# Multi-query attention with causal masks: where the mask is applied

## The reference

```python
Q = (x @ Wq + bq).reshape(B, S, H, Dh).transpose(0, 2, 1, 3)   # B, S = 8, 512; H, Dh = 16, 8
K = x @ Wk + bk
V = x @ Wv + bv
A = einsum('bhqd,bkd->bhqk', Q, K)
A = where(tril(ones((S, S))), A, -inf)
P = softmax(A / sqrt(Dh), axis=-1)
O = einsum('bhqk,bkd->bhqd', P, V)
return O.transpose(0, 2, 1, 3).reshape(B, S, H * Dh) @ Wo + bo
```

## Time and profile before

| | before |
|---|---|
| median of 3 runs | 4353.27 us |
| profiled execution | 4353.17 us, span 4351.2 us |
| PE, DVE, ACT, POOL busy | 3755.5, 3342.7, 2178.1, 2945.7 us |
| attention stage | about 49 to 676 us, a batch every 78.9 us |
| mean granted PE clock | 0.96 |

### The profile page before, as it was taken

How to read it: one execution, slowest core, us unless ns; L and a number is a source line. 1 busy time by engine, 2 the same in 40 slices (tenths; PEclk the granted TensorE clock), 3 DMA queues, 4 the chain that set the end, 5 groups by cost and what they waited for, 6 DMA issues and landing times. The chain is left out here.

```text
span 4351.2 us, 158059 instructions
## 1 busy us (share of the span) xinstructions
PE 3755.5 (86%) x67688; PEld 2914.4 (67%) x67880; DVE 3342.7 (77%) x4810; ACT 2178.1 (50%) x2712; POOL 2945.7 (68%) x1281
## 2 busy tenths in 40 slices
PE   6888895889888898988898988989888989889985
PEld 4555554767676776766777767777666767777773
DVE  3454555888887888887888878888878788888884
ACT  3444443555554555554555545555545555555552
POOL 1101005888887877887888878788877788788872
PEclk9999997999999999999999999999999999999997
DMA  1000001222223222222222232222222222222221
GB/s 48 3 5 2 5 3 43 77 61 61 61 62 80 57 62 61 61 66 72 61 61 62 61 80 60 61 61 60 66 73 60 61 61 62 66 62 61 61 61 50
DMA packets 162246, 239.83 MB, mean 55 GB/s; under 512 B 42258, under 2 KB 60632, under 8 KB 161496
## 3 DMA queue, kind: packets, MB, share of 16 engines
q1 hardware_dynamic: 161624, 230.00, 20.5%
HBM read 21.00 MB, written 4.19 MB: 6 GB/s over the span
## 5 line engine op out<-in xcount | busy, mean ns | idle before, releaser
L1054 POOL TENSOR_TENSOR norms<-sumsb,minus_half 128x16 f32<-128x16 f32 x384 | 1145.3, 2983 | 238.9 <-DVE sumsb L1381 212.1
L1058 POOL TENSOR_TENSOR by_cos<-by_cos,by_sin 128x1024 f32<-128x1024 f32 x384 | 917.9, 2390 | 356.9 <-DVE by_sin L1373 351.7
L1279 ACT ACTIVATE squares<-proj 128x1024 f32<-128x1024 f32 x384 | 393.9, 1026 | 743.5 <-PE proj L1121 743.5
L1064 POOL TENSOR_TENSOR by_cos<-by_cos,norms 128x1024 f32<-128x1024 f32 x384 | 743.9, 1937 | 32.6
L1371 DVE TENSOR_TENSOR by_cos<-proj,turns 128x1024 f32<-128x1024 f32 x384 | 467.9, 1218 | 300.8 <-ACT squares L1279 281.1
L1119 PE MATMUL proj<-qkv_hi,xs_hib 128*128 128x512 f32 x1152 | 528.1, 458 | 57.6 <-DVE by_sin L1373 42.3
L1377 DVE TENSOR_REDUCE sumsb<-squares 128x16 f32<-128x1024 f32 x384 | 465.1, 1211 | 11.9 <-ACT squares L1279 10.3
L1120 PE MATMUL proj<-qkv_lo,xs_hib 128*128 128x512 f32 x1152 | 471.5, 409 | 0.0
L1121 PE MATMUL proj<-qkv_hi,xs_lob 128*128 128x512 f32 x1152 | 470.8, 409 | 0.0
L1373 DVE TENSOR_TENSOR by_sin<-proj,turns 128x1024 f32<-128x1024 f32 x384 | 465.6, 1213 | 0.0
L1128 PE MATMUL ring<-ident,by_cos 128*128 128x128 f32 x3072 | 410.4, 277 | 0.0
(11 more groups left out here) (173 smaller groups left out, 7346.7 us busy)
## 6 DMA issues: line engine op xcount, KB each, us to landing
v_win<-vb SPq DMA_DIRECT2D x1152, 130.0 KB
v_win<-vb SPq DMA_DIRECT2D x768, 65.0 KB
in_qkv<-L_ffn_Wqkv SPq DMA_DIRECT2D x12, 768.0 KB
wo<-L_ffn_Wo SPq DMA_DIRECT2D x6, 512.0 KB, 4.1
x_tok<-L_attn_x SPq DMA_DIRECT2D x8, 256.0 KB, 4.6
residual<-x_tok SPq DMA_DIRECT2D x8, 256.0 KB, 2.0
o_x<-residual SPq DMA_DIRECT2D x1, 2048.0 KB, 7.9
out<-o_x SPq DMA_DIRECT2D x8, 256.0 KB, 2.3
```

The lines of the kernel that those rows point to most:

```text
L1054: nc.gpsimd.tensor_tensor(norms[:, t % 2, j, :], sums[:, t % 2, j, :], c["minus_half"][:, 0:H], ALU.pow).then_inc(e[f"{w_}_norm"].sem, 1)
L1058: nc.gpsimd.tensor_tensor(by_cos[:, j, :], by_cos[:, j, :], by_sin[:, j, :], ALU.add).then_inc(e[f"{w_}_added"].sem, 1)
L1064: nc.gpsimd.tensor_tensor(heads, heads, norms[:, t % 2, j, :].unsqueeze(2).broadcast_to([P, H, DH]), ALU.mult).then_inc(e[f"{w_}_ready"].s ...
```

## The change

The causal mask leaves PE in both products. For the maxima, `mask_qk` becomes 512 columns wide, zero but for its last 128, and DVE adds its last n columns to the score inside the instruction that takes the maximum; the masked scores go to a scratch tile `a_unused` that nothing reads. Each maximum now has a second wait, on the one two before it, and an increment of a semaphore `a_dve_ready` in front. For the transposed scores no mask is added before the exponential; when a group's 12 exponentials are done, POOL sets the part under the diagonal of the first 128 columns of each block to zero in `probs`, one selection per key tile over the 4 heads, and PE's V of key tile kt waits for selection kt. On POOL's queue group 0's selections stand before inverse deviation 2 of the batch before, group 1's before inverse deviation 0, and group 3's behind `keys_again`. One selection and one memset less build the constants.

```diff
-            sp.wait_ge(selected, 9)
+            sp.wait_ge(selected, 8)
...
-            select(c["mask_qk"][:, :], [[-1, P]], ALU.is_ge, 0, MASKED, 1)
-            select(c["mask_kq"][:, :], [[1, P]], ALU.is_ge, 0, MASKED, -1)
+            select(c["mask_qk"][:, S - P:S], [[-1, P]], ALU.is_ge, 0, MASKED, 1)
...
+            def causal(b, g):
+
+                pool.wait_ge(e["exp"].sem, e["exp"].at(3 * PER_GROUP * (g + 1), b))
+                pool.sem_inc(pool_ready, 1)
+                for kt in range(TILES):
+                    own = probs[:, g % 2, :, PROB_AT[kt]:PROB_AT[kt] + P]
+                    nc.gpsimd.affine_select(out=own, in_=own, compare_op=ALU.is_ge, fill=0.0, base=0,
+                                            pattern=[[0, PER_GROUP], [1, P]], channel_multiplier=-1)\
+                        .then_inc(e["causal"].sem, 1)
+
             def sequence(b, first=False, last=False):
                 if not first:
                     inverse_deviation(1, b - 1)
+                causal(b, 0)
+                if not first:
                     inverse_deviation(2, b - 1)
+                causal(b, 1)
                 if not last:
                     inverse_deviation(0, b + 1)
+                causal(b, 2)
+                if not last:
                     keys_again(b + 1)
+                causal(b, 3)
...
-                nc.tensor.matmul(out[:, 0:n], qT0[:, g, qt * P:(qt + 1) * P], kT[:, i, 0:n], start=True, stop=False)
-                nc.tensor.matmul(out[:, n - P:n], ident_bf[:, :], c["mask_qk"][:, :],
-                                 start=False, stop=True).then_inc(e["s_full"].sem, 1)
+                nc.tensor.matmul(out[:, 0:n], qT0[:, g, qt * P:(qt + 1) * P], kT[:, i, 0:n], start=True,
+                                 stop=True).then_inc(e["s_full"].sem, 1)
...
-                    nc.tensor.matmul(out[:, at:at + n], kT1[:, i, kt * P:(kt + 1) * P], qT1[:, g, kt * P:S],
-                                     start=True, stop=False)
-                    last = nc.tensor.matmul(out[:, at:at + P], ident_bf[:, :], c["mask_kq"][:, :],
-                                            start=False, stop=True)
+                    last = nc.tensor.matmul(out[:, at:at + n], kT1[:, i, kt * P:(kt + 1) * P], qT1[:, g, kt * P:S],
+                                            start=True, stop=True)
...
             def weighted_values(b, g, kt):
 
+                pe.wait_ge(e["causal"].sem, e["causal"].at(TILES * g + kt + 1, b))
                 if kt == 0:
-                    pe.wait_ge(e["exp"].sem, e["exp"].at(3 * PER_GROUP * (g + 1), b))
...
                     dve.wait_ge(e["s_full"].sem, e["s_full"].at(s + 1, b))
-                    nc.vector.tensor_reduce(row_max[:, qt, h:h + 1], score[s % 2][:, 0:P * (qt + 1)], AX.X,
-                                            ALU.max).then_inc(e["s_max"].sem, 1)
+                    dve.wait_ge(e["s_max"].sem, e["s_max"].at(s - 1, b))
+                    dve.sem_inc(dve_ready, 1)
+                    n = P * (qt + 1)
+                    nc.vector.tensor_tensor_reduce(unused[:, s % 2, 0:n], score[s % 2][:, 0:n], c["mask_qk"][:, S - n:S], 1.0,
+                                                   LOWEST, ALU.add, ALU.max, accum_out=row_max[:, qt, h:h + 1])\
+                        .then_inc(e["s_max"].sem, 1)
```

More of the change, by code:

```diff
@@ L43 @@
 QK_SCALE = 8.0
+LOWEST = float(np.finfo(np.float32).min)
 MASKED = -1e30
@@ L112, in _ @@
             nc.vector.memset(c["mask_qk"][:, :], 0.0)
-            nc.vector.memset(c["mask_kq"][:, :], 0.0)
             nc.vector.memset(c["mask_win"][0:WINDOW, :], 0.0)
@@ L176, in mqa_events @@
         "st_full": Events(sem("a_st_full"), 3 * MQA_H), "exp": Events(sem("a_exp"), 3 * MQA_H),
+        "causal": Events(sem("a_causal"), TILES * GROUPS),
         "pv_full": Events(sem("a_pv_full"), GROUPS), "pv": Events(sem("a_pv"), GROUPS),
@@ L214, in mqa_stage @@
         o, y = sb("a_ob", [P, TILES, D]), sb("a_yb", [P, TILES, D])
-        carrier = sb("a_carrier", [P, 1])
+        carrier, unused = sb("a_carrier", [P, 1]), sb("a_unused", [P, 2, S], BF16)
         turn = [bank("a_turn0"), bank("a_turn1")]
@@ L222, in mqa_stage @@
         stored = ctx.enter_context(nc.semaphore("a_stored"))
+        pool_ready = ctx.enter_context(nc.semaphore("a_pool_ready"))
+        dve_ready = ctx.enter_context(nc.semaphore("a_dve_ready"))
         block = ctx.enter_context(nc.Block())
@@ L1573, in program @@
             "ones": sb("ones", [P, P]), "mean_of": sb("mean_of", [P, P]), "minus_half": sb("minus_half", [P, H]), "least": sb("least", [P, 2, H]),
-            "mask_qk": sb("mask_qk", [P, P], BF16), "mask_kq": sb("mask_kq", [P, P], BF16),
+            "mask_qk": sb("mask_qk", [P, S], BF16),
             "mask_win": sb("mask_win", [P, 512], BF16), "mask_first": sb("mask_first", [P, 512], BF16),
```

## The result

The changed kernel takes 4380.77 us, the median of 8 runs (4371.25 to 4397.99), against 4355.05 us before on the same chip; the ratio is 1.0054, 95% interval [1.0033, 1.0074]. It is slower, by half a percent. The forecast was 4372 us, slower with a chance of 0.60. The profiled execution took 4386.02 us, its span is 4384.1.

The account below looks back on a forecast made before the run. By busy shares PE bounds the attention cycle, though timelines show PE and DVE alternating over two score banks. Per cycle -4.3+5.4+1.45 = +2.55; with the ends +18.8 on 4353.17 us, forecast 4372 us, range 4325 to 4425.

Parts of the forecast that it names:

- part 1: Mask matmuls taken off PE in the attention stage: 4.3 us a cycle gained.
- part 3: Selections on POOL: hidden except in group 3 at the batch boundary, where V starts late: +1.45 us a cycle.
- part 2: Mask inside DVE's maximum, with readout, second wait and increment: 5.4 us a cycle lost.
- rival 3: PE, left idle longer at the batch boundary, stays at half clock for more 4-us slices: 4380 to 4400 us; chance 0.12.
- rival 1: Faster: DVE's readout, waits and increment cost nothing; cycle -2.85 us, with the ends -25, 4328 us; chance 0.28.
- a: Extra DVE time per maximum for the separate 128x1 result: 0.06 us, bounds 0 and 0.18.
- w: Second wait and increment before each maximum, counting where DVE stands ready for a score: 0.20 us, bounds 0 and 0.4.
- with nothing else changed: Condition under which PE's gains from removed masks were summed along the attention stage's path, 4.3 us a cycle.
- Rival 4: Masks cost PE next to nothing on any path, weight loads being the bound: gain 1.5 instead of 4.3, 4392 us; chance 0.06.
- Holds no edited line: The span outside the attention stage, some 3675 us, has no edited line, so the change can touch only some 630 us.
- Rival 2: Much slower by DVE: readout 0.18 us, wait and increment 0.4; cycle +10, in all +78, 4431 us; chance 0.12.
- the pair at 0.38: Sign: time from a 512-column matmul with its mask to the next, 0.38 us, becomes about 0.23 where PE is busy.

Follow-up runs that it names:

- plain_max: The changed kernel with DVE's maximum as a plain reduction, without mask, second wait or increment; 4316.74 us, ratio to before 0.9921.
- pm_keep_T: Against before, only the score mask is left out, maximum a plain reduction; transposed mask stays on PE, nothing on POOL; 4473.97 us, ratio 1.0276.
- pool_only: The changed kernel with the score mask back on PE and the plain maximum on DVE, selections still on POOL; 4393.03 us, ratio to before 1.0094.
- order: The changed kernel with POOL's selections for group 3 ahead of the key copy; 4370.11 us, ratio to before 1.0027.

## Why the prediction was right or wrong

The sign was right. That the time came within 9 us is partly luck. The stage was forecast 18.8 us longer and became 40.7 longer: part 1 with part 3 gave 16 us less than forecast, part 2 cost 6 more. The second stage, taken as fixed, gave 7.8 back in the profile, and the medians differ by 25.7. The 4380.77 us also lie at the low end of rival 3's 4380 to 4400, and by the estimate under part 1 it is mostly rival 3's mechanism that made the stage longer than forecast.

- **Part 2, the DVE maximum: right, a little small.** Forecast 5.4 us a cycle, some 44 with the ends (18.8 above rival 1's -25); measured 49.9, after against plain_max, 6.9 a cycle. A part of that is clock again: cycles at a like clock are 80.60 (0.79) and 84.70 us (0.80), 78.10 and 82.21 (both 0.85), a difference of 4.1 each, and 78.57 (0.83) and 83.60 (0.84), 5.0. Its signs came out: DVE starts 0.22 us after a score it waited for (forecast 0.2), a head of maxima takes 2.25 us (2.3; the same head in plain_max 1.97), and the main part costs nothing extra. The readout a was 0.083 us, taken as 0.06. The Trainium skill's rule of two instructions (VectorE: DVE Perf Modes, section Two Vector instructions with no wait between them) is what the trace of after shows, with 512 readouts behind 512 maxima. Of w's 0.20 the wait is the small part and the increment the large one; the forecast had put half on each.
- **Part 1, masks off PE: the failed step.** With part 3 it was to give 25 us, and gave 9.2 (678.0 to 668.8), 0.3 a cycle instead of 2.85. PE's share was right. In the changed kernel unmasked matmuls follow each other as forecast:

```profile
253.06 0.40 PE L335 MATMUL a_scoreT<-a_qT,a_kT 128*128 128x512 f32 x1
253.30 0.22 PE L324 MATMUL a_score<-a_kT,a_qT 128*128 128x128 f32 x1
253.36 0.45 PE L335 MATMUL a_scoreT<-a_qT,a_kT 128*128 128x384 f32 x2
```

  A row of 512 columns makes room after 0.24 us (forecast 0.23, 0.38 with its mask), one of 128 after 0.06. The time freed was not kept: "with nothing else changed" was the phrase that failed. The clock changed, from 0.95 to 0.86 in plain_max and 0.83 in after. This was rival 3's mechanism, given 0.12 and priced at one or two 4-us slices; it came as 27 to 44 us of half clock in each of the three cycles shown, where before has 3 to 10. It acts together with part 2, whose waits thin PE's work further.

  Is it enough for the missing 16 us? plain_max has 0.86 over its six cycles and before 0.96, some 22 and 6 us of half clock a cycle; at 0.24 us for each that is 3.7 us a cycle, 22 over the six. So the clock is enough, and without its fall the cycle would have gained about 4 us where 2.85 was forecast; plain_max's cycle at 0.91 (75.70) is already shorter than before's at 0.98 (76.87). This is an estimate; no run holds the clock up without adding work. The kernels with half of the masks fit it: pm_keep_T's first cycle takes 76.14 us at 0.93, before's 79.18 at 0.94, while its others are at 0.89 to 0.91 and take 78.4 to 78.8. pool_only gains less, 77.83 at 0.93, and waits 7.3 us for selections in its stage. Rival 4's number for part 1, 1.5 a cycle, is nearer to what came of it, but by another cause.
- **Part 3, the selections on POOL: right place, half the size.** One takes 0.60 us (four in 2.39) instead of 0.75; V waited 1.1 us on average and 1.43 at most instead of 1.9, and order gives back 5.0 and 4.3 us, neither firm, where 7 times 1.45, 10, was forecast. The other groups are hidden, as said. The waits of the changed kernel's stage say both:

```profile
PE a_pv_bank L348 <- POOL a_probs L289: 7.9, 7, 1.4
DVE a_ob L637 <- POOL a_rstdb L271: 1.1, 1, 1.1
```

  PE waited seven times, once per boundary, 7.9 us in all. The wait for an inverse deviation is the one before had, also 1.1 us, once.
- **"Holds no edited line": the step that was missing.** The forecast took the second stage as fixed. Over these kernels it ran from 3642 to 3800 us, more than any term of the sum. In after it happened to be 7.8 us shorter; in pm_keep_T, 127 us longer, it would have turned any forecast from the stage over. The range held the time by its width, not because this was in it.
- **Rivals.** Rival 1 needed a and w at nothing: a is 0.083, and DVE starts 0.18 us later than in plain_max (0.22 against 0.04). Rival 2's prices (0.18, 0.4) weren't reached. Rival 4's test, the pair at 0.38 becoming 0.24, went against it.

## What to carry to other kernels

Where two engines pass one buffer pair back and forth, an instruction in front of the waiting one can count once per pass: here an increment of a semaphore in front of DVE's maximum cost more (31.8 us) than the mask inside it (11.5), so look for a way to order the writes that needs none. Before work is taken off TensorE, look how near its clock is to falling, and count the freed time only if it doesn't. If the clock moved, compare cycles of the two kernels at the same granted clock: here that showed a gain that the totals hid. Compare the stage that was edited, not only the whole: moving PE's program ahead of the long second stage moved that stage by 110 us, more than the edit is worth.

## What the hardware did that was not expected

- Shifting PE's program by 384 instructions changed an untouched stage from 3782.6 to 3672.5 us; PE's waits for issue at one line there went from 121.6 to 74.8 us.
- An increment between wait and instruction delays DVE's start behind a score from 0.04 to 0.18 us; a second wait alone doesn't (0.04).
- 1024 matmuls whose results are thrown away raised the mean granted clock of the stage from 0.83 to 0.94, and its six cycles fell from 84.6 to 82.5 us on average.
- Cycles of one trace, with the same instructions, take 75.7 us at a granted clock of 0.91 and 80.6 at 0.79.
